# Attention scores in two groups of 64 TensorE columns, with a mask for 16 tokens

## The chip, the cores and the metric

The kernel runs on one core of a Trainium2 chip. The metric is the device time of one execution in microseconds, the median of several runs. The engines are named as in the profile: PE is TensorE, PEld its weight loads, DVE VectorE, ACT ScalarE, POOL GpSimd, SP SyncE (here only a DMA queue).

## The reference

One block on x of shape (8, 1024, 256), float32, so 8192 tokens of width 256. Layer norm gives xn. An attention branch and a mixture of experts (8 experts, the best 2 of each token) both read xn, and the output is x + s * silu(moe). The part that matters here is the attention, which runs over the 4 heads *inside* each token, not over tokens:

```
q = (x @ Wq + bq).reshape(b, s, h, d)      # h = 4 heads, d = 256
k = (x @ Wk + bk).reshape(b, s, h, d)
v = (x @ Wv + bv).reshape(b, s, h, d)
scores = (einsum('bshd,bsgd->bshg', q*cos, k*cos) + einsum('bshd,bsgd->bshg', q*sin, k*sin)) / 16
attn = softmax(scores, axis=-1)            # 4 x 4 numbers for each token
out = einsum('bshg,bsgd->bshd', attn, v)
```

So every token needs 16 dot products of length 512 (cosine and sine part), each between one of its own queries and one of its own keys.

## The kernel before

The tokens go through in 16 quarters of 512 tokens (loop variable `q`, constant `NQ`), the first four (`QE = 4`) ahead of the experts, the other twelve behind them. A quarter has 24 steps `c` on PE. Steps 0 to 15 (L1075, fp32r, 6 matmuls of 512 columns) make the rotated queries and keys. ACT (L814) and DVE (L1590) each write one half of them (cosine, sine) into `QT`, which holds queries as columns (token, head) and keys as columns (head g, token). Steps 16 to 23 (L1086, fp32) make the values folded with Wo, which leave through `u_d` in memory and come back as `US`. Behind the 24 steps come four score groups `n = 4q .. 4q+3` of 128 tokens each (`scores`, L1022), 64 in the kernel.

A score group has four blocks `c` of 32 tokens. In a block the stationary operand is 128 columns of queries (32 tokens times 4 heads), the moving operand 128 columns of keys (4 heads times 32 tokens), in four accumulating fp32 matmuls. Of the 128 x 128 products only those between equal tokens are wanted. DVE multiplies the bank with a mask (`soft_a`, L1478, `maskt` has a one where query row and key column are of one token), sums over the tokens (L1482), takes the maximum and subtracts it (L1483, L1484); ACT takes the exponential (L835); DVE normalises (`soft_b`, L1489 to L1491). In the next quarter `spread` (L1496 to L1505) and `biased` (L1516) get the attention and the values ready, and PE multiplies them in `mix` (L1043: four matmuls, each with 32 stationary columns, one for each 32 PSUM partitions), taken in behind steps 18, 20, 22 and 23.

The score groups alternate between two PSUM banks (`pS`, banks 4 and 5). Group n waits until DVE's mask product of group n-2 is done (`s_sm1`). The steps c go round five banks (`ring`), so step c+5 waits until ACT and DVE have emptied the bank of step c. Each engine works off its own program in order. In quarters 1 to 3 PE also adds up the experts' token lists (`place`, L1053, bf16), POOL and DVE make their operands (L588, L1547, L1551). POOL makes `XTJ` for the next quarter (L574) while the scores run, and behind the experts it also sums the experts' outputs (L658 to L665) and ends with L673 and L674; ACT's silu for it is L801, placed at step 18, and L797 for the quarters of the first half that are finished later. L921 is the router's matmul at the start: 32 stationary columns, 256 moving, one after another. In the last quarter `mix` also follows the scores directly.

Of the kernel before, what the change touches and what calls it, by code (L numbers as in the profile page):

```python
# [9 lines left out]
ALU = mybir.AluOpType  # L10
ACT = mybir.ActivationFunctionType
AX = mybir.AxisListType

NB, S, D, H = 8, 1024, 256, 4
# [22 lines left out]
def program(nc, x, phase, Wq, bq, Wk, bk, Wv, bv, Wo, bo, rw, rb, temp, wg, wp, wo, out):  # L37
    ctx = ExitStack()

    def sb(name, shape, dt=F32):  # L40
        return ctx.enter_context(nc.sbuf_tensor(name, shape, dt))
# [4 lines left out]
    with ctx:  # L46
# [30 lines left out]
        QT = WM[:, 0:16384].rearrange("p (x c n) -> p x c n", x=4, c=2)  # L77
# [14 lines left out]
        TM = sb("TM", [128, 512])  # L92
# [32 lines left out]
        upper = AUX[:, 8064:8192]  # L125
        bo_b = sb("bo_b", [128, D])
        maskt = sb("maskt", [128, 32])
        mask8 = sb("mask8", [128, 8])
        maskr = sb("maskr", [128, 8])
        vec = sb("vec", [128, 4, 8])  # L130
# [28 lines left out]
        SS = sb("SS", [128, 2, 16])  # L159
# [13 lines left out]
        pXT, pS, pD = ps[3], ps[4:6], ps[7]  # L173
# [709 lines left out]
        def _(e):  # L883
# [3 lines left out]
            for k in range(2):  # L887
                mm = e.transpose(bP[:, 32 + 8 * k:40 + 8 * k], rwN[:, 128 * k:128 * k + 128], ident[0:8, 0:8])
# [96 lines left out]
            for j in range(18):  # L985
# [4 lines left out]
                for c in range(2):  # L990
                    if j < 16:
                        k, g = j // 8, j // 2 % 4
                        mm = e.matmul(mb[j % 5][:, :], WvT[:, 2 * g + c, 128 * k:128 * k + 128], wo_r[:, c, :, :],  # L993
                                      start=(c == 0), stop=(c == 1))
                    else:
                        mm = e.matmul(mb[j % 5][0:4, :], bvT[:, c:8:2], wo_r[:, c, :, :],
                                      start=(c == 0), stop=(c == 1))
# [17 lines left out]
            def scores(n):  # L1015
                if n >= 2:
                    e.wait_ge(s_sm1, n - 1)
                for c in range(4):
                    col = 128 * (4 * (n % 4) + c)
                    for x in range(2):  # L1020
                        for h in range(2):
                            mm = e.matmul(pS[n % 2][:, 128 * c:128 * c + 128].rearrange("p (g t) -> p g t", g=H),  # L1022
                                          QT[:, x, h, col:col + 128],
                                          QT[:, 2 + x, h, :].rearrange("p (g t) -> p g t", g=H)[:, :, col // 4:col // 4 + 32],
                                          start=(x == h == 0), stop=(x == h == 1))
                mm.then_inc(s_s, 1)

            def mix(n):
# [160 lines left out]
        def _(e):  # L1189
# [25 lines left out]
            e.wait_ge(s_const, 1)  # L1215
            e.tensor_reduce(maskt[:, :], ident[:, :].rearrange("p (t h) -> p t h", h=H), AX.X, ALU.add)
            ch(e.tensor_reduce(maskr[:, :], ident[:, :].rearrange("p (r a) -> p r a", a=16), AX.X, ALU.add))
            ch(e.tensor_reduce(mask8[:, :], maskt[:, :].rearrange("p (a t) -> p t a", t=8), AX.X, ALU.add))


# [250 lines left out]
            def g4(a, n):  # L1471
                return a[:, n % 2, :].rearrange("p (c g) -> p c g", g=H)

            diag = maskt[:, None, :].broadcast_to([128, 4 * H, 32])

            def soft_a(n):
                e.wait_ge(s_s, n + 1)
                e.tensor_tensor(TM[:, :].rearrange("p (x t) -> p x t", t=32),  # L1478
                                pS[n % 2][:, :].rearrange("p (x t) -> p x t", t=32), diag,
                                ALU.mult).then_inc(s_sm1, 1)  # L1480
                e.wait_ge(s_sm1, n + 1)
                ch(e.tensor_reduce(SS[:, n % 2, :], TM[:, :].rearrange("p (x t) -> p x t", t=32), AX.X, ALU.add))  # L1482
                ch(e.tensor_reduce(sx[:, 0, :], g4(SS, n), AX.X, ALU.max))  # L1483
                e.tensor_tensor(g4(SS, n), g4(SS, n), sx[:, 0, :, None].broadcast_to([128, 4, 4]),  # L1484
                                ALU.subtract).then_inc(s_sub, 1)
# [193 lines left out]
```

## Time and profile before

| | us |
|---|---|
| median of the runs | 1698.37 (1698.24 to 1698.8) |
| the profiled execution | 1698.34 |
| its span in the trace | 1696.6 |
| PE busy | 1643.0 (97%) |
| DVE busy | 988.6 (58%) |
| POOL busy | 785.1 (46%) |
| ACT busy | 733.4 (43%) |
| quarters 0 to 3 | about 128 to 354 |
| experts | about 354 to 1035 |
| quarters 4 to 15 | about 1035 to 1694 |

PE is busy nearly always. A matmul's busy time in the trace goes on beyond its own columns (matmuls overlap in the engine), so what a group of matmuls costs is read from the chain that ended last, or from the distance between starts, and not from the mean of one. An fp32 matmul of the program stands in the trace as two matmuls, each with its own weight load; so 1024 score matmuls are 2048 rows.

### The profile page before, as it was taken

The page shows a single profiled execution, that of the slowest core. Times are in us where ns is not written, and L with a number is a line of the kernel's source. Part 1 is how long each engine was busy: PE and PEld are TensorE (multiplying, and loading weights), DVE is VectorE, ACT ScalarE, POOL GpSimd, SP SyncE. Part 2 cuts the span into 40 slices and gives each one's busy share as a digit, 9 for nine tenths or more (in the row PEclk, how much of TensorE's full clock was granted, in tenths as well). Part 3 has the DMA queues.
Part 4 walks back from the last instruction along what each step waited for, and adds up shares of the span by engine and source line. Part 5 has one row for each costly group of instructions (what it writes and reads, how often), then busy time and mean ns, then how long its engine had stood idle before and what let it go on. Part 6 is the DMA issues. An engine that isn't in the chain of part 4 may idle for free.

```text
span 1696.6 us, 28609 instructions
## 1 busy us (share of the span) xinstructions
PE 1643.0 (97%) x9360; PEld 1276.8 (75%) x9360; DVE 988.6 (58%) x1879; ACT 733.4 (43%) x1205; POOL 785.1 (46%) x945
## 2 busy tenths in 40 slices
PE   5998999989999999999999999999999999999998
PEld 3556676578888888888888888776877668776785
DVE  7568988843333333333333335768777786777766
ACT  5773432513333333333333335355454564535542
POOL 4647577614333433343433442534544646345362
PEclk9999999999999999999999999999999999999998
DMA  9988733162313131313111412424556345552354
GB/s 331 398 319 311 265 107 125 63 263 89 128 51 128 56 124 57 125 57 125 54 54 57 156 54 84 162 101 160 180 180 199 124 155 178 189 182 97 126 168 137
DMA packets 162662, 250.96 MB, mean 148 GB/s; under 512 B 13928, under 2 KB 121248, under 8 KB 161376
## 3 DMA queue, kind: packets, MB, share of 16 engines
q1 hardware_dynamic: 147904, 211.47, 35.8%
q0 software_dynamic: 12960, 35.41, 6.3%
q10 hardware_dynamic: 1664, 2.26, 0.4%
q8 instruction: 88, 1.44, 0.3%
q14 instruction: 46, 0.38, 0.1%
HBM read 149.58 MB, written 99.50 MB: 147 GB/s over the span
## 4 chain that ended last, share of the span: by engine, by line
PE 88%; DVE 6%; DMA 4%; ACT 1%; issue 1%; POOL 0%; ACTq 0%; SPq 0%; DVEq 0%
PE ps L1140 21%; PE ps L1075 19%; PE ps L1022 13%; PE ps L1086 12%; PE ps L1159 10%; PE ps L1149 3%; DMA AUX<-xn_d,AUX 3%; PE ps L1043 2%; PE ps L1122 2%; PE ps L993 2%; PE ps L921 1%; PE ps L911 1%; PE ps L977 1%; DVE WM L1590 1%; DMA WR<-w_d 1%
## 5 line engine op out<-in xcount | busy, mean ns | idle before, releaser
L1140 PE MATMUL ps<-WR,FR 128*128 x1620 | 414.6, 406 | 5.1 <-issue 3.3
L1140 PEld LDWEIGHTS ps<-WR,FR 128*128 128x128 f32 x1620 | 300.7, 192 | 65.6 <-issue 6.7
L646 POOL DMA_INDIRECT y_d<-AUX x135 | 133.7, 990 | 371.6 <-ACT AUX L865 371.6
L1650 DVE TENSOR_TENSOR AUX<-AUX,ps 128x512 f32<-128x512 f32 x135 | 92.9, 688 | 352.7 <-ACT AUX L853 352.7
L814 ACT ACTIVATE WM<-ps,bcs,trig 128x512 f32<-128x512 f32 x256 | 255.7, 1018 | 88.2 <-PE ps L1075 80.5
L1590 DVE TENSOR_SCALAR WM<-ps,vec,trig 128x512 f32<-128x512 f32 x256 | 246.2, 995 | 62.4 <-ACT WM L814 61.8
L1022 PE MATMUL ps<-WM 128*128 128x128 f32 x2048 | 236.3, 277 | 7.2 <-DVE TM L1478 7.2
L1022 PEld LDWEIGHTS ps<-WM 128*128 128x128 f32 x2048 | 232.0, 193 | 14.7 <-DVE TM L1478 8.0
L1086 PE MATMUL ps<-WM,XTJ 128*128 128x512 f32 x512 | 237.1, 600 | 0.0
L853 ACT ACTIVATE AUX<-ps 128x512 f32<-128x512 f32 x135 | 80.9, 599 | 329.0 <-PE ps L1140 329.0
L1159 PE MATMUL ps<-WR,ABR 128*128 x1080 | 209.5, 292 | 0.0
L1075 PE MATMUL ps<-XH,WH 128*128 128x512 f32 x512 | 204.7, 400 | 4.9 <-issue 3.8
L1075 PE MATMUL ps<-XH,WL 128*128 128x512 f32 x512 | 200.3, 391 | 0.0
L1075 PE MATMUL ps<-XL,WH 128*128 128x512 f32 x512 | 200.2, 391 | 0.0
L642 POOL DMA_INDIRECT AUX<-xn_d,AUX x135 | 132.0, 978 | 77.1 <-issue 39.2
L1159 PEld LDWEIGHTS ps<-WR,ABR 128*128 128x128 f32 x1080 | 165.5, 190 | 0.0
L1086 PEld LDWEIGHTS ps<-WM,XTJ 128*128 128x128 f32 x512 | 91.6, 190 | 96.6 <-issue 94.2
L658 POOL TENSOR_TENSOR AUX<-AUX,GP 128x256 f32<-128x256 f32 x128 | 81.9, 677 | 158.1 <-DMA AUX<-in_L_attn_x_dram 155.9
L1159 PE MATMUL ps<-WR,FR 128*128 x540 | 152.0, 281 | 0.0
L821 ACT ACTIVATE UN<-ps 128x512 f32<-128x512 f32 x128 | 76.2, 595 | 138.7 <-PE ps L1086 135.6
L1075 PEld LDWEIGHTS ps<-XH,WH 128*128 128x128 f32 x512 | 96.8, 189 | 25.0 <-issue 4.8
L835 ACT ACTIVATE SE<-SS 128x16 f32<-128x16 f32 x64 | 13.8, 216 | 232.4 <-DVE SS L1484 232.3
(237 smaller groups left out, 2282.5 us busy)
## 6 DMA issues: line engine op xcount, KB each, us to landing
US<-u_d SPq DMA_DIRECT2D x63, 512.0 KB, 4.7
u_d<-UN SPq DMA_DIRECT2D x120, 256.0 KB, 2.0
WR<-w_d SPq DMA_DIRECT2D x8, 3072.0 KB
AUX<-y_d SPq DMA_DIRECT2D x32, 512.0 KB, 5.7
WM<-in_L_attn_x_dram SPq DMA_DIRECT2D x16, 512.0 KB, 9.6
xn_d<-WM SPq DMA_DIRECT2D x32, 256.0 KB, 6.8
w_d<-USR SPq DMA_DIRECT2D x16, 512.0 KB, 5.1
AUX<-xn_d SPq DMA_DIRECT2D x16, 512.0 KB, 6.5
```

The lines of the kernel that those rows point to most:

```text
L642: e.indirect_dma_start(XG[:, m % 2, :], None, xn_d, bass.IndirectOffsetOnAxis(gidx[:, m:m + 1], 0)).then_inc(s_g[m % 2], 16)
L646: e.indirect_dma_start(y_d, bass.IndirectOffsetOnAxis(toks[:, m - 5:m - 4], 0), YS[:, (m - 5) % 2, :], None).then_inc(s_y[(m - 5) % 2], 16)
L658: ins = e.tensor_tensor(y[:, i, :], y[:, i, :], GP[:, i, k, q, None].broadcast_to([128, D]), ALU.mult)
L814: e.activation(rotated(2 * x, i), b, ACT.Identity, bias=bcs[:, x, 0, i:i + 1], scale=trig[:, 0, i:i + 1]).then_inc(s_ca, 1)
L853: e.activation(GR[:, :], mG[m % 2][:, :], ACT.Relu).then_inc(s_gr, 1)
L1022: mm = e.matmul(pS[n % 2][:, 128 * c:128 * c + 128].rearrange("p (g t) -> p g t", g=H), QT[:, x, h, col:col + 128], QT[:, 2 + x, h, :].rea ...
L1075: mm = e.matmul(b[:, :], w[:, k, 128 * c:128 * c + 128], xx[:, k, :], start=(k == 0 and w is WH and xx is XH), stop=(k == 1 and w is WL))
L1086: mm = e.matmul(b[:, :], XTJ[:, k, a // 2, :], M_s[:, k, 512 * a:512 * a + 512], start=(k == 0), stop=(k == 1))
L1140: mm = e.matmul(b[:, :], x, WR[:, bass.ds(off[m] + (2048 * z + 1024 * a + 512 * k), 512)], start=(k == 0 and x is xh and z == 0), stop=(k ...
L1159: mm = e.matmul(mY[m % 2][:, 0:256], x, WR[:, bass.ds(off[m] + (4096 + 1024 * z + 256 * c), 256)], start=(c == 0 and x is hh and z == 0), ...
L1590: e.tensor_scalar(rotated(2 * x + 1, i), ps[bank(24 * q + c)][:, :], bqk[:, x, i:i + 1], trig[:, 1, i:i + 1], ALU.add, ALU.mult).then_inc( ...
L1650: e.tensor_tensor(HS[:, m % 2, :], GR[:, :], mP[m % 2][:, :], ALU.mult).then_inc(s_h, 1)
```

## The change

Each block of 32 tokens is split in two halves of 16 tokens. The stationary operand of a half is 64 query columns, the moving operand 64 key columns (4 heads times 16 tokens), and the result goes to PSUM partitions 0 to 63 for the first half and 64 to 127 for the second, at the same 64 columns. The two halves alternate matmul by matmul. A bank then holds 256 columns of scores in place of 512, the mask has 16 columns in place of 32, and DVE's mask product and sum read 256 columns.

```diff
+        mask16 = sb("mask16", [128, 16])
...
                 for c in range(4):
-                    col = 128 * (4 * (n % 4) + c)
                     for x in range(2):
                         for h in range(2):
-                            mm = e.matmul(pS[n % 2][:, 128 * c:128 * c + 128].rearrange("p (g t) -> p g t", g=H),
-                                          QT[:, x, h, col:col + 128],
-                                          QT[:, 2 + x, h, :].rearrange("p (g t) -> p g t", g=H)[:, :, col // 4:col // 4 + 32],
-                                          start=(x == h == 0), stop=(x == h == 1))
+                            for a in range(2):
+                                row = 64 * a
+                                col = 128 * (4 * (n % 4) + c) + row
+                                mm = e.matmul(pS[n % 2][row:row + 64, 64 * c:64 * c + 64].rearrange("p (g t) -> p g t", g=H),
+                                              QT[:, x, h, col:col + 64],
+                                              QT[:, 2 + x, h, :].rearrange("p (g t) -> p g t", g=H)[:, :, col // 4:col // 4 + 16],
+                                              start=(x == h == 0), stop=(x == h == 1))
                 mm.then_inc(s_s, 1)
...
+            e.tensor_tensor(mask16[:, :], maskt[:, 0:16], maskt[:, 16:32], ALU.add)
...
-            diag = maskt[:, None, :].broadcast_to([128, 4 * H, 32])
+            diag = mask16[:, None, :].broadcast_to([128, 4 * H, 16])
...
-                e.tensor_tensor(TM[:, :].rearrange("p (x t) -> p x t", t=32),
-                                pS[n % 2][:, :].rearrange("p (x t) -> p x t", t=32), diag,
+                e.tensor_tensor(TM[:, 0:256].rearrange("p (x t) -> p x t", t=16),
+                                pS[n % 2][:, 0:256].rearrange("p (x t) -> p x t", t=16), diag,
                                 ALU.mult).then_inc(s_sm1, 1)
...
-                ch(e.tensor_reduce(SS[:, n % 2, :], TM[:, :].rearrange("p (x t) -> p x t", t=32), AX.X, ALU.add))
+                ch(e.tensor_reduce(SS[:, n % 2, :], TM[:, 0:256].rearrange("p (x t) -> p x t", t=16), AX.X, ALU.add))
```

On PE, the score groups of a quarter behind the experts stand between the last `mix` and the first step of the next quarter. Before:

```order
L1043 MATMUL ps<-US,AT 32x256 x3
L1022 MATMUL ps<-WM 128x128 [waits s_sm1,s_cd,s_ca]
L1022 MATMUL ps<-WM 128x128 x15
L1022 MATMUL ps<-WM 128x128 [waits s_sm1]
L1022 MATMUL ps<-WM 128x128 x15
L1022 MATMUL ps<-WM 128x128 [waits s_sm1]
L1022 MATMUL ps<-WM 128x128 x15
L1022 MATMUL ps<-WM 128x128 [waits s_sm1]
L1022 MATMUL ps<-WM 128x128 x15
L1075 MATMUL ps<-XH,WH 128x512 [waits s_ca,s_cd,s_xtd,s_xtc]
```

The same place on PE with the change (line numbers are three higher there):

```order
L1046 MATMUL ps<-US,AT 32x256 x3
L1025 MATMUL ps<-WM 64x64 [waits s_sm1,s_cd,s_ca]
L1025 MATMUL ps<-WM 64x64 x31
L1025 MATMUL ps<-WM 64x64 [waits s_sm1]
L1025 MATMUL ps<-WM 64x64 x31
L1025 MATMUL ps<-WM 64x64 [waits s_sm1]
L1025 MATMUL ps<-WM 64x64 x31
L1025 MATMUL ps<-WM 64x64 [waits s_sm1]
L1025 MATMUL ps<-WM 64x64 x31
L1078 MATMUL ps<-XH,WH 128x512 [waits s_ca,s_cd,s_xtd,s_xtc]
```

Nothing moved: each group has 32 matmuls of 64 x 64 where it had 16 of 128 x 128, behind the same waits.

On DVE, one group's mask product to the end of the softmax of the group ahead of it. Before:

```order
L1478 TENSOR_TENSOR TM<-ps,maskt 128x512 [waits s_s]
L1482 TENSOR_REDUCE SS<-TM 128x16 [waits s_sm1]
L1483 TENSOR_REDUCE sx<-SS 128x4 [waits s_vc]
L1484 TENSOR_TENSOR SS<-SS,sx 128x16 [waits s_vc]
L1489 TENSOR_REDUCE sx<-SE 128x4 [waits s_exp]
L1490 RECIPROCAL sx<-sx 128x4 [waits s_vc]
L1491 TENSOR_TENSOR SA<-SE,sx 128x16 [waits s_vc]
```

The same place on DVE with the change:

```order
L1482 TENSOR_TENSOR TM<-ps,mask 128x256 [waits s_s]
L1486 TENSOR_REDUCE SS<-TM 128x16 [waits s_sm1]
L1487 TENSOR_REDUCE sx<-SS 128x4 [waits s_vc]
L1488 TENSOR_TENSOR SS<-SS,sx 128x16 [waits s_vc]
L1493 TENSOR_REDUCE sx<-SE 128x4 [waits s_exp]
L1494 RECIPROCAL sx<-sx 128x4 [waits s_vc]
L1495 TENSOR_TENSOR SA<-SE,sx 128x16 [waits s_vc]
```

The order is the same, the first two read half as many columns. One small DVE instruction is added at the start of the program (the mask). Nothing changes on ACT, POOL and SP.

## Rows read from the trace of the kernel before

**Rows 1.** The page: busy time, and the chain that ended last.

```profile
PE 1643.0 (97%) x9360; PEld 1276.8 (75%) x9360; DVE 988.6 (58%) x1879; ACT 733.4 (43%) x1205; POOL 785.1 (46%) x945
...
PE 88%; DVE 6%; DMA 4%; ACT 1%; issue 1%; POOL 0%; ACTq 0%; SPq 0%; DVEq 0%
PE ps L1140 21%; PE ps L1075 19%; PE ps L1022 13%; PE ps L1086 12%; PE ps L1159 10%; PE ps L1149 3%; DMA AUX<-xn_d,AUX 3%; PE ps L1043 2%; PE ps L1122 2%; PE ps L993 2%; PE ps L921 1%; PE ps L911 1%; PE ps L977 1%; DVE WM L1590 1%; DMA WR<-w_d 1%
```

**Rows 2.** The chain over one quarter: start us, us, what.

```profile
1131.86 14.49 PE ps L1022 x128
1146.35 21.79 PE ps L1075 x96
1168.14 3.43 PE ps L1086 x8
...
1173.73 0.57 PE ps L1043 x8
```

**Rows 3.** Groups of instructions on PE and PEld, by shape (stationary, then moving).

```profile
L1022 PE MATMUL ps<-WM 128*128 128x128 f32 x2048 | 236.3, 277 | 7.2 <-DVE TM L1478 7.2
...
L1022 PEld LDWEIGHTS ps<-WM 128*128 128x128 f32 x2048 | 232.0, 193 | 14.7 <-DVE TM L1478 8.0 <-issue 5.8 <-ACT UN L821 0.8
...
L1043 PEld LDWEIGHTS ps<-US,AT 128*32 128x32 f32 x504 | 10.1, 108 | 43.1 <-issue 21.2 <-DVE AT L1505 20.8
...
L952 PEld LDWEIGHTS ps<-ident,AUX 128*64 128x64 f32 x3 | 0.3, 110 | 1.7 <-DVE AUX L1339 1.2 <-issue 0.5
```

**Rows 4.** Timeline of PE and PEld around one mix: start us, us.

```profile
1119.95 0.64 PE L1043 MATMUL ps<-US,AT 128*32 128x256 f32 x8
...
1119.94 0.16 PEld L1043 LDWEIGHTS ps<-US,AT 128*32 128x32 f32 x8 [0.76 <-issue]
```

**Rows 5.** The chain at the router and at one place.

```profile
62.41 0.98 PE ps L921 x4
...
224.83 0.24 PE ps L1053 x4
```

**Rows 6.** Timeline of DVE over the quarter of rows 2.

```profile
1142.81 0.69 DVE L1478 TENSOR_TENSOR TM<-ps,maskt 128x512 f32<-128x512 f32 x1 [1.25 <-PE ps L1022]
...
1144.96 0.17 DVE L1491 TENSOR_TENSOR SA<-SE,sx 128x16 f32<-128x16 f32 x1
...
1149.64 3.33 DVE L1590 TENSOR_SCALAR WM<-ps,vec,trig 128x512 f32<-128x512 f32 x3 [0.42 <-ACT WM L814]
```

**Rows 7.** Timeline there, POOL and DVE at once.

```profile
1133.92 4.49 POOL L574 TENSOR_TENSOR XTJ<-XH,XL 128x256 f32<-128x256 f32 x4
...
1137.32 1.13 DVE L1484 TENSOR_TENSOR SS<-SS,sx 128x16 f32<-128x16 f32 x1
```

**Rows 8.** Groups of instructions on DVE.

```profile
L1478 DVE TENSOR_TENSOR TM<-ps,maskt 128x512 f32<-128x512 f32 x64 | 44.2, 690 | 88.1 <-PE ps L1022 88.1
L1482 DVE TENSOR_REDUCE SS<-TM 128x16 f32<-128x512 f32 x64 | 43.9, 686 | 2.2
L1527 DVE TENSOR_TENSOR AUX<-ps,bo_b 128x256 f32<-128x256 f32 x60 | 25.1, 418 | 29.3 <-PE ps L1043 23.5 <-DMA s_d<-AUX 5.6
```

**Rows 9.** The chain at scores of quarters 0, 3 and 15.

```profile
165.45 8.77 PE ps L1022 x64
...
346.82 7.41 PE ps L1022 x64
...
1668.16 7.36 PE ps L1022 x64
...
1680.43 3.78 PE ps L1022 x32
```

**Rows 10.** Busy us (and count) of each engine from 235.3 to 295.6, clock, DMA.

```profile
235.30:295.60 60.30, 60.30 (x370) 42.76 (x370) 53.44 (x110) 23.05 (x30) 49.80 (x51) 1.00 0.26 88
```

**Rows 11.** Timeline of POOL and ACT near step 18.

```profile
1169.21 2.88 POOL L665 TENSOR_TENSOR AUX<-AUX 128x256 f32<-128x256 f32 x4
...
1174.38 1.28 ACT L801 ACT_TABLE_LOAD   x1
```

## The prediction

> **What bounds the kernel now.** I read the page's busy times first: PE is busy for 97% of the span, and 88% of the chain that ended last is PE work, 13% of it the score matmuls [rows 1]. So a microsecond taken from PE counts, unless another engine is right behind. Then the chain over one quarter behind the experts: 14.49 us of scores, 21.79 us of steps 0 to 15, then the fp32 steps with the mixes among them [rows 2]. There is no piece of another engine in it: the quarter of 53.7 us is PE alone, eleven times over. The quarters ahead of the experts are another matter: from 235.3 to 295.6 DVE is busy for 53.44 of 60.3 us [rows 10], and in quarters 0 and 3 only two of the four groups are on the chain [rows 9], since the other two run while DVE does something longer.
>
> **What a score matmul costs.** A quarter has 128 pairs of a weight load and a matmul in 14.49 us, 113.2 ns a pair [rows 2]. Eight matmuls of 512 columns take 3.43 us [rows 2], 0.838 ns a column in fp32. So 128 moving columns stream for 107.2 ns, and 6.0 ns come on top. The weight load is as long as the stream: by its duration, 128 columns take 193 ns and 32 columns 108 [rows 3], 0.89 ns a column over a fixed 80. It lies beside the matmul of the pair ahead, or a pair could not take 113 ns.
>
> **The part that decides: do the two halves run at once?** The change makes 4096 pairs of 64 x 64 out of 2048 of 128 x 128. A half pair streams 64 columns, 53.6 ns, its load is about 57 ns by the same row arithmetic (a 64-column load had 110 ns [rows 3], less still, but that one loads for a transpose). With the 6.0 ns it takes 59.6 ns. One after the other, the 64 pairs of a group take 3.81 us, against 3.62 now: nothing won. Side by side, 32 pair times, 1.91 us: 1.71 us won in each group.
>
> The trace has a matmul split by columns already. A mix is eight pairs on four sets of 32 stationary columns, each with 256 moving columns. One such matmul streams 256 x 0.838 = 214 ns, and the router's matmuls of the same shape, all on one set of columns, take 0.98 us for four [rows 5], or 214 ns each with 0.12 us for the change of shape. Eight in a row would be 1.72 us. The mix takes 0.57 us on the chain [rows 2], its eight loads start within 0.16 us less the 108 ns of the last one, and its matmuls are over in 0.64 us by their modelled ends [rows 4]. So four sets of columns load and stream at once, at almost the full factor (2 x 214 = 428 ns and the change of shape). I take the same for two sets of 64. What it doesn't show is whether this holds for a long stream of pairs (64 a group, where a mix has eight), and with loads as long as the streams (in a mix the load is an eighth of the stream). Bounds for the pair time seen by the group: 28 ns (two at once and nearly no fixed cost, 1.8 us a group) and 59.6 ns (none at once). I take 29.8, nearest to the mix.
>
> A rule of the Trainium skill speaks against the change ("TensorE: Matmul & The Clock Gate", Part 3, what overlaps and what doesn't): weight loads overlap with matmuls in flight only where the row group differs, and here both halves use all rows. By it each load of 53.6 ns would stand outside the streams of all pairs. The rows on the present scores don't agree: PEld is busy for 232.0 us and PE for 236.3 us, together twice the time that the groups take, with all rows in use each time [rows 3].
>
> **DVE.** A mask product and a sum of 512 columns take 690 and 686 ns, a DVE operation from PSUM with 256 columns 418 [rows 8]. So both fall by 0.27 us, 0.54 a group, 35 us of DVE in all, mostly idle time today. For one group with the softmax of the last, DVE goes from 1142.81 to 1144.96 + 0.17 = 1145.13, 2.32 us [rows 6]; it falls to 1.78, still just under PE's new 1.91. But POOL's XTJ work runs for 4.49 us over the scores, and under it a small DVE operation took 1.13 us in place of 0.17 [rows 7]. With one or two such hits DVE ends the four groups about 3 us behind PE; then the evacuations of the next quarter begin. Today the first evacuation ends at 1149.64 + 3.33/3 = 1150.75, 4.4 us behind PE's start of step 0 at 1146.35 [rows 2, 6]. PE waits for it only at step 5, five steps of 21.79/16 = 1.36 us, 6.8 us, on. I expect the 4.4 to become about 5, so PE doesn't wait in most quarters. I take off 0.4 us a quarter for unlucky hits and for the two changes of shape (a change was 0.12 us above).
>
> **The sum**, by what is on the path:
> - Quarter 0: two groups on the chain [rows 9], 2 x 1.71 = 3.4 us. The other two hide behind DVE.
> - Quarters 1 and 2: eight groups, 13.7 us. DVE, 53.44 us busy, saves 2.2 and so has 51.3 us of work in a quarter that would shrink to some 53.4: 1 us each is lost to it. 11.7 us.
> - Quarter 3: two groups on the chain, 3.4 us. The experts: nothing, they only begin earlier.
> - Quarters 4 to 14: 44 groups, 75.3 us, less 11 x 0.4: 70.9 us.
> - Quarter 15: three groups on the chain (7.36 and 3.78 us [rows 9]), 5.1 us, and twice DVE's 0.54 where its softmax stands on the chain: 6.2 us.
>
> Together 95.6 us. The profiled execution took 1698.34 us, 0.03 from the median, so **about 1602 us**, 5.7% less.
>
> **Rivals.**
> *The halves run one after the other.* Then a pair has a fixed cost and 59 groups on the path take 3.81 us in place of 3.62: 11 us more, **1709 us**. The point where it turns is 56.6 ns a pair (3.62 us / 64). For it: the shortest distance between pairs on a whole array is 0.24 us / 4 = 60 ns, at the place matmuls [rows 5]. Against it: the mix. The Trainium skill has a price of this kind ("TensorE: Matmul & The Clock Gate", Part 1, on the missing 2.5 ns): about 62 ns of sequencer time for each matmul where hardware decoding is off. By it a group would take 64 x 62 = 4.0 us and the kernel about 1719 us; the eight loads of a mix that start within some 50 ns [rows 4] don't agree, though a queue filled while PE waited may stand behind that. 11%.
>
> *The halves stream at once but each load stands alone.* A pair of a half is then 53.6 + 53.6 + 6 = 113 ns, two at once, 32 x 113 = 3.62 us a group, as now: **1698 us**, perhaps 1 to 2 less by DVE. The load and stream of the present pairs overlap wholly [rows 3], so 3%. A partial overlap between this and mine, 1650 to 1695, another 4%.
>
> *Another engine becomes the bound.* The quarter shrinks to 46.9 us while DVE, ACT and POOL keep their waits. Two DVE hits more in each quarter put the first evacuation past the 6.8 us, and PE waits 1 to 2 us in each of 14 quarters. POOL's sums ended at 1172.09 and ACT's silu, which needs them, began at 1174.38 [rows 11]: a margin of 2.3 us, and PE's scores will bring step 18 forward by 6.9 us, POOL's inputs (behind ACT's L797, which follows the second softmax) only by about 3. ACT then waits some 1.6 us ahead of step 18's silu in four of the quarters. Steps 16 to 23 go round three banks of 1.72 us each, which should cover it. If it all sticks, 14 x 2 = 28 us of the gain go: **1630 us**. 14%.
>
> *Mine*, 68%: 1590 to 1615. The lower end is a pair time of 28 ns and no waits (59 x 1.8 + 1 = 107 us less), the upper one 1 us more lost in each quarter.
>
> **How the numbers follow.** Mine and the bound by another engine hold 82%; from 1589 to 1640 about 80% of all lies. A measurement can tell about 0.2%, 3.4 us, from no change. Faster by more: 68 + 14 + 4 and half of the 3%, about 87%. Within 0.2%: 2%. Slower: 11%.
>
> **What would show it.** In the chain a quarter's scores should be x256 in about 7.6 us, with pairs in two streams 60 ns apart each; the mean busy of a weight load about 135 ns. The quarter's distance should be about 47 us and PE's waits for DVE L1594 or ACT L815 (the evacuations, by their new line numbers) near nothing. DVE's mask product and sum should be near 0.42 us, and steps 0 to 15 still 21.8 us: if they are longer, the second engine has become late. A granted clock under 1.00 in the scores, where it is 1.00 now [rows 10], would be something I haven't priced. The prediction is wrong at its root if 256 pairs take 14 us or more.

## The result and the profile after

| | us |
|---|---|
| before, four runs on the same chip | 1698.59 (1698.24 to 1705.89) |
| changed | **1608.35** (1603.45 to 1611.25, four runs) |
| ratio | 0.9457, 95% interval 0.943 to 0.9484 |
| the profiled execution, changed | 1606.22, span 1604.5 |

The kernel got 90 us faster where 96 were forecast. The page of the changed kernel, busy times, the granted clock in 40 slices, and the chain that ended last by engine:

```profile
PE 1536.4 (96%) x11408; PEld 1169.5 (73%) x11408; DVE 974.2 (61%) x1880; ACT 730.0 (45%) x1205; POOL 794.2 (49%) x945
...
PEclk9999799989999999999999999999999999999999
...
PE 88%; DVE 5%; DMA 4%; ACT 1%; issue 1%; POOL 0%; ACTq 0%; SPq 0%; DVEq 0%
```

PE is still the bound, with 88% of the chain as in [rows 1], and no other engine has taken its place. The chain over the quarter that answers to [rows 2] (start us, us, what; L1025 is the score matmul, L1078 and L1089 are the steps):

```profile
1108.87 7.62 PE ps L1025 x256
1116.49 21.98 PE ps L1078 x96
1138.47 3.43 PE ps L1089 x8
```

Twice as many pairs in 7.62 us where 14.49 stood: 29.8 ns a pair as the quarter sees it. Steps 0 to 15 take 21.98 us, 0.19 more than before. The groups of the scores and of DVE's two operations on them, beside [rows 3, 8] (engine, operation, shape, count, busy us and mean ns, then idle time ahead and its releaser):

```profile
L1025 PE MATMUL ps<-WM 128*64 128x64 f32 x4096 | 130.9, 227 | 16.2 <-DVE TM L1482 15.6
...
L1025 PEld LDWEIGHTS ps<-WM 128*64 128x64 f32 x4096 | 127.1, 143 | 25.0 <-DVE TM L1482 16.1
```

```profile
L1486 DVE TENSOR_REDUCE SS<-TM 128x16 f32<-128x256 f32 x64 | 26.9, 420 | 2.2
L1482 DVE TENSOR_TENSOR TM<-ps,mask 128x256 f32<-128x256 f32 x64 | 26.8, 418 | 23.0 <-PE ps L1025 23.0
```

The mask product and the sum fell from 690 and 686 ns to 418 and 420, as forecast. What is new is the length of the scores' waits for the mask product: 15.6 us, 7.2 before [rows 3]. The timeline of PE in quarters 0 and 3 shows most of it, in the brackets:

```profile
165.31 6.58 PE L1025 MATMUL ps<-WM 128*64 128x64 f32 x128 [10.46 <-DVE TM L1482]
...
336.08 6.53 PE L1025 MATMUL ps<-WM 128*64 128x64 f32 x128 [4.42 <-DVE TM L1482]
```

and the engines over these two stretches and one of quarter 1 (busy us and count of PE, PEld, DVE, ACT and POOL, then the granted clock, DMA share, GB/s):

```profile
165.30:172.00 6.70, 6.70 (x129) 6.63 (x130) 5.97 (x18) 0.65 (x3) 6.08 (x7) 0.56 1.02 351
336.10:342.60 6.50, 6.50 (x129) 6.43 (x130) 3.89 (x17) 0.65 (x3) 0.41 (x1) 0.56 1.08 442
219.90:221.80 1.90, 1.90 (x64) 1.84 (x64) 0.07 (x1) 0.00 (x0) 1.34 (x2) 1.00 0.58 207
```

After a wait of 10.5 or 4.4 us, 128 pairs take 6.6 and 6.5 us at a mean granted clock of 0.56, mostly the lower level of 1.2 GHz, while 64 pairs in quarter 1 take 1.9 us at 1.00 (2.4 GHz).

Where the time came from, by the start of each quarter's scores in the traces. The second execution is that of the repeat further down:

| stretch | forecast | changed | repeat |
|---|---|---|---|
| to the scores of quarter 1 (quarter 0) | 3.4 | 1.2 | -2.2 |
| quarters 1 and 2 | 11.7 | 9.5 | 11.4 |
| from the scores of quarter 3 to the experts | 3.4 | 0.7 | -4.5 |
| experts | 0 | 4.9 | 3.1 |
| experts' end to the scores of quarter 4 | 0 | 0.0 | 0.0 |
| quarters 4 to 14 | 70.9 | **70.9** | **69.9** |
| quarter 15 | 6.2 | 4.9 | 4.9 |
| sum | 95.6 | 92.1 | 82.7 |

(Before, the scores of quarters 1, 2, 3, 4 and 15 start at 221.0, 279.9, 338.4, 1078.1 and 1668.1; changed, at 219.8, 274.8, 327.7, 1061.8 and 1580.9. The experts, from the start of their first L1140 matmul, L1143 with the change, to the start of the last, run from 359.7 to 1031.3 and from 348.3 to 1015.0.)

### The profile page after: what moved, and what is told of

It is laid out like the page before. It is cut to its first block, busy times and chain, and to the rows that moved or that the text cites. A ratio compares the mean times of both kernels' runs of the same rounds, so it can differ in the third digit from the quotient of the medians.

```text
span 1604.5 us, 32706 instructions
## 1 busy us (share of the span) xinstructions
PE 1536.4 (96%) x11408; PEld 1169.5 (73%) x11408; DVE 974.2 (61%) x1880; ACT 730.0 (45%) x1205; POOL 794.2 (49%) x945
## 4 chain that ended last, share of the span: by engine, by line
PE 88%; DVE 5%; DMA 4%; ACT 1%; issue 1%; POOL 0%; ACTq 0%; SPq 0%; DVEq 0%
PE ps L1143 21%; PE ps L1078 21%; PE ps L1089 13%; PE ps L1162 11%; PE ps L1025 7%; PE ps L1152 3%; DMA AUX<-xn_d,AUX 3%; PE ps L1046 2%; PE ps L1125 2%; PE ps L994 2%; PE ps L922 1%; PE ps L978 1%; PE ps L912 1%; DVE UN L1228 1%; DMA WR<-w_d 1%
## 5 line engine op out<-in xcount | busy, mean ns | idle before, releaser
L1143 PE MATMUL ps<-WR,FR 128*128 x1620 | 408.4, 401 | 5.7 <-issue 3.1
L1143 PEld LDWEIGHTS ps<-WR,FR 128*128 128x128 f32 x1620 | 296.6, 190 | 65.0 <-issue 7.6
L815 ACT ACTIVATE WM<-ps,bcs,trig 128x512 f32<-128x512 f32 x256 | 252.1, 1016 | 89.8 <-PE ps L1078 83.0
L1089 PE MATMUL ps<-WM,XTJ 128*128 128x512 f32 x512 | 237.1, 600 | 0.0
L1078 PE MATMUL ps<-XH,WH 128*128 128x512 f32 x512 | 205.8, 402 | 4.9 <-issue 3.8
L1078 PE MATMUL ps<-XH,WL 128*128 128x512 f32 x512 | 200.5, 392 | 0.0
L1078 PE MATMUL ps<-XL,WH 128*128 128x512 f32 x512 | 200.5, 392 | 0.0
L1089 PEld LDWEIGHTS ps<-WM,XTJ 128*128 128x128 f32 x512 | 91.6, 190 | 96.6 <-issue 92.5
L1162 PE MATMUL ps<-WR,FR 128*128 x540 | 152.0, 281 | 0.0
L1025 PE MATMUL ps<-WM 128*64 128x64 f32 x4096 | 130.9, 227 | 16.2 <-DVE TM L1482 15.6
L1025 PEld LDWEIGHTS ps<-WM 128*64 128x64 f32 x4096 | 127.1, 143 | 25.0 <-DVE TM L1482 16.1
L1078 PEld LDWEIGHTS ps<-XH,WH 128*128 128x128 f32 x512 | 97.0, 189 | 25.8 <-issue 4.9
L1635 DVE TENSOR_TENSOR FR<-ps,FR 128x256 fp32r<-128x256 f32 x135 | 57.3, 425 | 93.2 <-ACT FR L847 93.2
```

The source lines that it names most:

```text
L815: e.activation(rotated(2 * x, i), b, ACT.Identity, bias=bcs[:, x, 0, i:i + 1], scale=trig[:, 0, i:i + 1]).then_inc(s_ca, 1)
L1025: mm = e.matmul(pS[n % 2][row:row + 64, 64 * c:64 * c + 64].rearrange("p (g t) -> p g t", g=H), QT[:, x, h, col:col + 64], QT[:, 2 + x, h, ...
L1078: mm = e.matmul(b[:, :], w[:, k, 128 * c:128 * c + 128], xx[:, k, :], start=(k == 0 and w is WH and xx is XH), stop=(k == 1 and w is WL))
L1089: mm = e.matmul(b[:, :], XTJ[:, k, a // 2, :], M_s[:, k, 512 * a:512 * a + 512], start=(k == 0), stop=(k == 1))
L1143: mm = e.matmul(b[:, :], x, WR[:, bass.ds(off[m] + (2048 * z + 1024 * a + 512 * k), 512)], start=(k == 0 and x is xh and z == 0), stop=(k ...
L1162: mm = e.matmul(mY[m % 2][:, 0:256], x, WR[:, bass.ds(off[m] + (4096 + 1024 * z + 256 * c), 256)], start=(c == 0 and x is hh and z == 0), ...
```

## The experiments

My theory: nearly the whole gain is that the two column halves of the array load and stream at once, and the finer blocks alone bring nothing. DVE's smaller operations matter only where DVE bounds. The first four kernels change the two halves, the next two DVE's part alone, and the rest look into what was left over: the pace, the supply of instructions, and the clock.

**Both halves on one set of columns.**

```diff
-                    for x in range(2):
-                        for h in range(2):
-                            for a in range(2):
+                    for a in range(2):
+                        for x in range(2):
+                            for h in range(2):
...
-                                mm = e.matmul(pS[n % 2][row:row + 64, 64 * c:64 * c + 64]...
+                                mm = e.matmul(pS[n % 2][0:64, 256 * a + 64 * c:256 * a + 64 * c + 64]...
```

> The changed kernel, but both halves go to PSUM partitions 0 to 63 (the second half to columns 256 to 511), so both use the same 64 columns of the array, and the eight pairs of one half of a block stand ahead of those of the other. Partitions 64 to 127 get no scores, so the output isn't the reference's. Theory (the gain is two column sets at once, a pair on one set costs 53.6 + 6.0 = 59.6 ns): 256 pairs of a quarter take 15.3 us in the chain, 0.8 more than the 14.49 before the change, and the kernel about 1700 to 1710 us. Rival (smaller loads and streams overlap better in themselves, the column sets have nothing to do with it): the quarter's scores stay near 7.6 us and the kernel near 1608.

Measured: 1708.99 us (1708.87 to 1715.81), ratio to before 1.0073 (1.0045 to 1.0102). The chain has, for one quarter:

```profile
1243.98 15.07 PE ps L1025 x256
```

58.9 ns a pair, twice 29.4. Same pairs, same shapes, same DVE work, and the 90 us are gone. The edit changes two things, the column set and the order of the pairs; the next run has this order with the two sets kept, and its 9.52 us against 15.07 are the second set alone. So what brings the gain is that a second set of columns runs beside the first. The time is also that of the first rival (1709 us), had the halves not run at once.

**The order of the halves.** First eight pairs of one half and then eight of the other in each block, then all 32 of one half and all 32 of the other in each group.

```diff
                 for c in range(4):
-                    for x in range(2):
-                        for h in range(2):
-                            for a in range(2):
+                    for a in range(2):
+                        for x in range(2):
+                            for h in range(2):
```

(This is the first of the two; the second has `for a in range(2)` ahead of `for c in range(4)` as well.)

> The changed kernel with the loop over the halves outside the accumulation: eight pairs of the first half, then eight of the second, in each block. Theory A (each column set takes its pairs from the queue on its own, as the mixes suggest, where one set's pairs stand next to each other in the program): no difference, 7.6 us a quarter. Rival B (pairs start in program order, so the alternation is what makes them overlap): only the pairs at the seams overlap, 13 to 15.3 us a quarter, the kernel at 1680 to 1710 us.

> The same with the loop over the halves outermost: 32 pairs of the first half, then 32 of the second in each group. Theory A with unlimited view: 7.6 us a quarter. If PE can only look some pairs ahead, the second set starts late in each group and the quarter is between 7.6 and 15.3 us; the start of the second set's first pair against the first set's tells how far it sees. Rival B: 15.3 us.

Measured: by blocks 1636.05 us (1633.95 to 1638.15), ratio 0.963 (0.9597 to 0.9664); by groups 1692.89 (1690.95 to 1699.56), ratio 0.9974 (0.9956 to 0.9991). The chain of one quarter, by blocks and then by groups:

```profile
1215.12 9.52 PE ps L1025 x256
```

```profile
1237.81 13.82 PE ps L1025 x256
```

A quarter has 32 seams between halves in the first kernel and 8 in the second. Against the 15.07 us of one set each seam wins (15.07 - 9.52) / 32 = 0.173 us and (15.07 - 13.82) / 8 = 0.156 us, some three pairs of 59 ns. The single starts say the same: by blocks the second half's first pair starts when the first half has about three pairs left. So here the engine starts a pair of the other set no more than some three or four pairs ahead. By blocks neither expectation came true (7.6 us, or 13 to 15.3); by groups the one of a short view did. Against the kernel before, runs of eight pairs keep 62 of the 90 us and runs of 32 keep 5.5. Two sets of columns run at once all the time only if the program alternates them more finely than that.

**Four sets of 32 columns**, 8 tokens times 4 heads, mask of 8 tokens, 128 columns for DVE.

```diff
-                            for a in range(2):
-                                row = 64 * a
+                            for a in range(4):
+                                row = 32 * a
...
-                                mm = e.matmul(pS[n % 2][row:row + 64, 64 * c:64 * c + 64]...
-                                              QT[:, x, h, col:col + 64],
+                                mm = e.matmul(pS[n % 2][row:row + 32, 32 * c:32 * c + 32]...
+                                              QT[:, x, h, col:col + 32],
...
```

> The split taken one step on: four sets of 32 columns, 8 tokens times 4 heads, mask of 8 tokens (mask8, which is there already), DVE reads 128 columns. A pair streams 32 columns, 26.8 ns, with 6.0 on top 32.8; 32 of them in a row on each of four sets: 1.05 us a group against 1.91, 4.2 us a quarter against 7.62. If nothing else binds, 0.86 us x 59 groups = 50 us off 1608, about 1558 us. Rival (another engine binds): DVE needs about 1.78 - 0.28 = 1.5 us for a group, four groups 6 us and more, so it ends the scores 2 to 3 us later behind PE than now; then PE waits at step 5 and the gain shrinks to 15 to 35 us, 1573 to 1593. Rival (a lowest distance between starts of pairs): with 512 pairs a quarter, at 15 ns each 7.7 us and no gain, 1608.

Measured: 1754.3 us (1745.31 to 1764.78), ratio 1.0332 (1.0298 to 1.0366). Slower than before, and my theory missed it. The chain over one quarter's 512 pairs (of pairs that run side by side it counts only some):

```profile
1264.19 1.43 PE ps L1024 x97
1265.62 2.68 issue
1268.31 1.93 PE ps L1024 x100
1270.23 2.36 issue
1272.60 1.93 PE ps L1024 x102
1274.53 2.64 issue
1277.16 1.50 PE ps L1024 x92
```

The group of these matmuls and the queue of instruction fetches between 1260 and 1285 us (packets, MB, share):

```profile
L1024 PE MATMUL ps<-WM 128*32 128x32 f32 x8192 | 104.0, 216 | 162.6 <-issue 149.2 <-DVE TM L1480 13.3
```

```profile
q8 instruction: 4, 0.07, 1.5%
```

PE stands still for 149 us with nothing that it waits for in the program. By the timeline the bursts are of 163, 128, 128 and 93 pairs. They start 4.29 and 4.56 us apart where they are of 128 pairs (256 instructions). The four fetches are of 16 KB each, which is 64 bytes for each of 256 instructions; they start at 1265.1, 1269.5, 1274.7 and 1279.1, and each burst behind a gap begins 2.5 to 3.2 us after the start of a fetch. Over the whole program this queue moves 88 pieces in the kernel before, 104 in the changed kernel and 136 in this one, one more for every 128 pairs. So a burst is one fetched piece, and the pace is that of the fetches: 4.3 us for 128 pairs in this quarter, 34 ns a pair, slower than the 29.8 ns at which two sets use them up. Over the kernel the next burst starts 3.5 to 7.9 us behind the start of one of 128 pairs, 5.4 in the median. The Trainium skill has the same unit ("Advanced Engine Details and Errata", ISA Cache: 16 KB, 256 instructions), and the trace agrees; it gives no rate of supply.

While instructions are at hand the four sets do what the theory said. The quarter shown and the next one begin at a clock of 1.00:

```profile
1264.01 1.61 PE L1024 MATMUL ps<-WM 128*32 128x32 f32 x163
...
1319.42 2.21 PE L1024 MATMUL ps<-WM 128*32 128x32 f32 x235
```

The 235 starts of the second burst lie within 2.02 us, 8.6 ns a pair, and once they have settled two pairs start every 16.7 ns: 8.3 ns a pair, 33 ns on each of the four sets, where the theory had 32.8. (The expectation of the run with 32 moving columns, below, takes these 16.7 ns for the distance of single pairs; they are that of two.) Behind the gaps of the quarter shown the granted clock is 0.50, and 128 pairs start within 1.69 us, 13.3 ns a pair, 53 ns on a set. So the rival of a lowest distance between pairs did not come true either: the loss is the supply of instructions, and the clock behind the gaps: steps 0 to 15, which follow, take 23.1 to 24.3 us in place of 21.98 in the three quarters from 1109 to 1247.

**DVE's part alone**, both ways: the new matmuls with the old 512 columns for DVE (the diff is of the first, shortened), and the old matmuls with 256 columns for DVE.

```diff
-            diag = mask16[:, None, :].broadcast_to([128, 4 * H, 16])
+            diag = maskt[:, None, :].broadcast_to([128, 4 * H, 32])
...
-                e.tensor_tensor(TM[:, 0:256].rearrange("p (x t) -> p x t", t=16),
+                e.tensor_tensor(TM[:, :].rearrange("p (x t) -> p x t", t=32),
...
```

> The changed PE order, but DVE's mask product and sum go over all 512 columns of the bank with the 32-token mask, as before the change; half of what they read isn't scores of this group, so the output isn't the reference's. It prices DVE's part of the change with the fast PE. Theory (DVE is late at the end of the scores but within the five banks): DVE ends four groups 2.2 us later, 4.4 + about 2.7 us behind PE's step 0, past the 6.8 us in some quarters; 0.5 to 2 us a quarter, 1615 to 1640 us. Rival (DVE has so much room that its part gives nothing): 1606 to 1612.

> The kernel before with DVE's part of the change alone: mask product and sum over 256 columns, PE as before (half of the scores unread, output isn't the reference's). PE bounds the quarters, so DVE's 0.54 us a group counts only where its softmax is on the chain (quarter 15, twice, and quarters 0 to 3): 1695 to 1698 us, 0 to 3 us less than before. If it gave 10 us or more, DVE would have been a second bound all along.

Measured: 1620.08 us (1618.54 to 1628.73), ratio 0.954 (0.952 to 0.956), for the new matmuls alone; 1696.22 (1692.59 to 1704.58), ratio 1.0 (0.998 to 1.002), for DVE's part alone. In the first, the chain of a late quarter is the changed kernel's:

```profile
1222.45 7.62 PE ps L1025 x256
1230.07 22.01 PE ps L1078 x96
```

and the quarters behind the experts stay 47.0 to 48.2 us apart. I had looked for a cost in each of them; there is none, so the margin of DVE behind PE is wider there than I thought. Quarters 1 and 2 take 59.4 and 55.5 us from scores to scores in place of 55.0 and 52.9: 7 us, where DVE's extra work in them is 8 x 0.54 = 4.3 us. That is where DVE bounds. The rest can't be placed: the profiled execution is this kernel's longest (1628.73 us), and 8.5 us of its distance lie in the experts' stage (675.2 us against 666.7), which the edit doesn't touch. By itself DVE's part is worth nothing that can be measured. On top of the new matmuls it is worth some 8 to 12 us between the medians (1620.08 against 1611.62 and 1608.35): the expected total (1615 to 1640) came, but not in the expected place.

**Every score matmul twice** (512 pairs a quarter), to see how far the instructions reach.

```diff
-                for c in range(4):
+                for c in [*range(4)] * 2:
```

> The changed kernel with each group's matmuls issued twice over (same results), so 512 pairs of 64 x 64 a quarter. With two column sets and instructions always at hand: 15.2 us a quarter, 29.8 ns a pair. If the supply of instructions is what gave the kernel with four sets its gaps (about 100 pairs, then 2 to 6 us with nothing to do, 4.4 us and more from run to run of pairs): one 16 KB piece of program holds 128 pairs, and at 4.4 us a piece 512 pairs need 17 to 18 us, with gaps of no named cause behind the first 200 to 300 pairs. Rival (the gaps belong to four column sets): no gaps here.

Measured: 1758.42 us, one run. The chain over one quarter:

```profile
1204.72 10.29 PE ps L1025 x347
1215.02 1.39 issue
1216.41 3.95 PE ps L1025 x128
1220.36 3.63 issue
1223.99 1.32 PE ps L1025 x37
```

347 pairs run through, then PE waits for each piece of 128. At 29.7 ns (10.29 / 347) a piece is used up in 3.95 us, and the next comes 7.6 us after the last. The gaps do not belong to four column sets. The changed kernel asks for 256 pairs and then has long steps: about the size of the reserve. In two of its late quarters PE stops for 0.05 and 0.20 us behind 235 and 251 pairs, and the repeat further down stops at the same two places, for 0.67 and 0.55 us:

```profile
1250.92 7.03 PE ps L1025 x235
...
1258.00 0.85 PE ps L1025 x21
```

**The clock after the long waits.** PE waits in quarters 0 and 3 for DVE. First I filled the wait with repeated scores (group 1 six times, group 13 three times).

```diff
-                for c in range(4):
+                for c in [*range(4)] * {1: 6, 13: 3}.get(n, 1):
```

> The changed kernel, where group 1 is computed six times over and group 13 three times (the same results written again), in the two places where PE waits 10.5 and 4.4 us for DVE with the granted clock at 0.56 behind it. Theory (these waits cost the clock, and with it most of what the change could give in quarters 0 and 3): the 128 pairs behind each wait take 3.8 us in place of 6.58 and 6.53, and the kernel gains 3 to 5.5 us on the changed kernel, about 1603. Rival (DVE is right behind there, so a faster PE only waits for it): the pairs take 3.8 us but the time stays at 1606 to 1611.

Measured: 1625.9 us (1618.85 to 1628.85), ratio 0.9563 (0.954 to 0.9587), slower than the changed kernel. Its chain in quarter 0:

```profile
154.35 5.40 PE ps L1025 x180
159.75 1.64 issue
161.39 3.95 PE ps L1025 x128
165.35 0.60 issue
```

The pairs run at full pace, but their number drains the supply, so the run doesn't tell what the clock alone costs. The scores of quarter 1 come 68.93 us after those of quarter 0, as in the changed kernel (68.90); 12.8 us of what is lost lie in the experts' stage (679.5 us against 666.7), which the edit doesn't touch. Then I filled the waits with few and wide matmuls, 11 and 4 of 512 columns, next to the changed kernel again, unaltered.

```diff
                         scores(4 * q + i)
+                        if i == 1 and q in (0, 3):
+                            e.wait_ge(s_ca, 24 * q + 24)
+                            for _ in range(11 if q == 0 else 4):
+                                e.matmul(ps[0][:, :], QT[:, 0, 0, 0:128], QT[:, 2, 0, 0:512], start=True, stop=True)
```

> The changed kernel once more, beside the next one on the same chip, to have its spread. Its four runs were 1603.45 to 1611.25. Theory: the spread comes from the experts' stage, where the weights of the next expert arrive beside the gathers: each of seven switches delays one or two steps of PE, 666 to 680 us in the profiles so far; the second half should again have quarters of 47.0 to 47.8 us. Median 1603 to 1614.

> The changed kernel with 11 fp32 matmuls of 512 columns behind group 1 and 4 behind group 13, written to a bank that is free there and read by nobody. They fill PE's two waits for DVE with 30 pairs in place of the 832 of the run before, which ran out of instructions (gaps of 1.6, 0.6, 0.3 and 1.7 us) and so mixed two things. Theory: the clock stays up, the 128 pairs behind each wait take 3.8 us in place of 6.5, and without the gaps the kernel is 3 to 5.5 us faster than the changed kernel beside it. Rival: DVE is next there, the 2.7 us turn into waits for DVE behind the scores, and the time is the same within 2 us.

Measured: the changed kernel again 1611.62 us (1605.46 to 1619.97), ratio 0.9481 (0.9451 to 0.9511), as expected, with late quarters of 47.0 to 48.2 us; with the wide matmuls 1622.55 (1617.26 to 1627.95), ratio 0.9556 (0.9535 to 0.9577). The chain of the second in quarter 0, and ahead of the experts:

```profile
168.45 3.95 PE ps L1025 x128
```

```profile
332.80 10.25 DMA AUX<-xn_d,AUX
...
343.59 6.26 PE ps L1065 x32
```

and ahead of the experts in the repeat:

```profile
335.07 10.77 DMA AUX<-xn_d,AUX
...
346.64 6.67 PE ps L1065 x32
```

Neither expectation gave the time: it is neither 3 to 5.5 us less than the repeat's nor the same. In quarter 0 the theory holds: with PE kept at work 128 pairs take 3.95 us at a clock of 1.00 in place of 6.58, and the scores of quarter 1 come 66.2 us after those of quarter 0, not 68.6 to 68.9. In quarter 3 the pairs take 3.95 us too, and nothing is won: PE then waits 3.9 us for the experts' first transfer, the clock is at 0.57 behind it, and L1065 takes 6.26 us. It takes 3.51 us in the changed kernel's first trace, at 1.00. So the wait is only moved, and which of the pieces runs at half clock differs between executions; that is a part of the runs' spread. That the kernel as a whole is 11 us slower in the median is not explained by this: its profiled execution is its fastest (1617.26) and has a span only 1.6 us above that of the repeat's. It stays open.

**The pace of a set.** 32 moving columns in place of 64, and 32 stationary columns in place of 64, one run each.

```diff
-                                mm = e.matmul(pS[n % 2][row:row + 64, 64 * c:64 * c + 64].rearrange("p (g t) -> p g t", g=H),
+                                mm = e.matmul(pS[n % 2][row:row + 64, 64 * c:64 * c + 32].rearrange("p (g t) -> p g t", g=2),
...
-                                              QT[:, 2 + x, h, :].rearrange("p (g t) -> p g t", g=H)[:, :, col // 4:col // 4 + 16],
+                                              QT[:, 2 + x, h, :].rearrange("p (g t) -> p g t", g=H)[:, 0:2, col // 4:col // 4 + 16],
```

```diff
-                                mm = e.matmul(pS[n % 2][row:row + 64, 64 * c:64 * c + 64].rearrange("p (g t) -> p g t", g=H),
-                                              QT[:, x, h, col:col + 64],
+                                mm = e.matmul(pS[n % 2][row:row + 32, 64 * c:64 * c + 64].rearrange("p (g t) -> p g t", g=H),
+                                              QT[:, x, h, col:col + 32],
```

> The changed kernel, but each score matmul moves 32 key columns (two of the four heads g) over the same 64 stationary columns; half of the scores are left out, so the output isn't the reference's. It parts load from stream. Theory (in a pair on one column set the weight load, 64 columns at 0.84 ns and some 5 ns, sets the pace, and the stream lies beneath it): still 58 ns a pair on each set, 7.6 us a quarter. Rival (the stream sets it): about 32 ns a pair on each set, so 4.1 us a quarter, or near 16.7 ns a pair as four sets had it within their runs, 4.3 us.

> The changed kernel, but each score matmul has 32 stationary query columns (the first 8 tokens of each half) and 64 moving ones; half of the scores are left out, so the output isn't the reference's. If the load alone sets the pace it falls to about 32 ns a pair on each set (4.1 us a quarter, if instructions are at hand; with 128 pairs to a piece of 16 KB and 4.4 us a piece, gaps again and some 7 to 9 us). If the stream sets it too, 7.6 us and no gaps.

Measured: 1616.79 and 1600.06 us. A quarter's scores in the chain, moving 32 and then stationary 32:

```profile
1211.13 7.59 PE ps L1025 x256
```

```profile
1202.24 7.14 PE ps L1025 x256
```

Half the moving columns change nothing (29.6 ns a pair, 59.3 for a set), as the theory had it: the load of 64 columns sets the pace there. The stationary run lies between its two expectations. Half the stationary columns bring 6% (27.9 ns, 55.8 for a set), though the mean load of quarters 4 to 15 is shorter by 28 ns (110 against 138): now the stream of 64 sets it. The bursts of the four sets have 32 on both sides, and there a set's pair takes 33 ns at full clock. So in these three shapes and in the changed kernel's a set's pair lasts as long as the longer of load and stream, at the 0.838 ns a column of the prediction (53.6 ns for 64, 26.8 for 32), and 2 to 7 ns more. A shortest distance of some 56 to 60 ns between pairs, whatever the columns, which the two runs by themselves would allow, does not agree with the 33 ns. Two sets with 32 on both sides were not run.

## Why the prediction was right, point by point

**The two halves at once: right.** I had argued it from eight pairs in 0.57 us [rows 2, 4, 5] and took 29.8 ns a pair, 1.91 us a group. Measured: 7.62 / 256 = 29.8 ns, in a stream of 256 pairs with loads as long as the streams. One set of columns gives 15.07 us, which shows the cause. The Trainium skill's rule that I set against it ("TensorE: Matmul & The Clock Gate", Part 3) doesn't hold in these rows: loads and streams that use all 128 rows overlap. What that argument left out is a condition: for the full gain the halves must alternate within three or four pairs. With runs of 32, 13.82 of the 15.07 us stay.

**Fixed cost of 6 ns and the price for each column: right, with a condition.** The sum 53.6 + 6.0 hit the pace of 59.5 ns. The prediction adds the 6 ns to the stream because load and stream are of one length. The longer of the two counts: 59.3 ns with half the moving columns, where the stream alone would give 33, and 55.8 with half the stationary ones. For pairs of 32 x 32 the same sum gives 32.8 ns, and the bursts of four sets have 33. What spoils that kernel, 3.3% slower than before, is a term that the sum doesn't have, the supply of instructions. The Trainium skill ("TensorEngine Tiling (Array Packing)", Theoretical Speedup) gives up to a factor of 4 for a dimension of 32 or less. Within a burst the four sets do run side by side; over the 512 pairs of a quarter no run here shows it, since they take 13 to 19 us against the 7.62 of two sets.

**DVE: right.** Both operations as forecast. The first evacuation of the quarter whose step 0 is at 1116.49 ends at 1120.91 + 5.25/5 = 1121.96, 5.5 us behind it where about 5 were forecast, inside the 6.8 us:

```profile
1120.91 5.25 DVE L1594 TENSOR_SCALAR WM<-ps,vec,trig 128x512 f32<-128x512 f32 x5 [0.16 <-ACT WM L815]
```

There is no wait for an evacuation in quarters 4 to 14. The rival "another engine becomes the bound" did not come true.

**Quarters 4 to 14: right, 70.9 of 70.9**, with the small loss from another source, so that the exact hit is in part luck. I took off 0.4 us a quarter for DVE's unlucky hits and the changes of shape. What is there is 0.19 us a quarter at the change from scores to steps: the steps take 21.98 us in the chain against 21.79, though their own starts keep their distances but for 0.02 us. 21.98 or a little more also stands in the kernels with one set, with the other orders and with DVE's 512 columns, and 21.79 in the one with DVE's part alone, so it goes with the split matmuls. The other part is 2.5 us in all, nearly all of it in three quarters, where PE has gaps of up to 0.7 us called "issue". Those within the scores, behind 235 and 251 pairs, fit the supply of instructions; those ahead of a mix have no cause that I can name.

**Quarters 1 and 2: 9.5 and 11.4 of 11.7.** The allowance for DVE was right in one execution, 2 us short in the other. In both the chain leaves PE for other engines, which before the change it hardly did. In the changed kernel's first trace, between the scores of quarters 1 and 2:

```profile
232.92 1.27 ACT WM L815
...
235.27 3.49 DVE OH L1551
...
270.64 2.65 DMA s_d<-AUX
```

DVE's 53.44 us in [rows 10] had said that this stage has little slack. The 60.3 us of that row are also 1.4 us more than a quarter (58.9 from scores to scores), so the room beside DVE was smaller than the sum took it.

**Quarters 0 and 3: the terms that were mis-sized.** The step was "two groups on the chain, 2 x 1.71 = 3.4 us" for each. Measured: 1.2 and 0.7 us, and less in the repeat. In quarter 0 even the 1.2 is in part chance, since the executions differ by 1.0 and -2.7 us before its scores start; from scores to scores it takes 68.9 and 68.6 us, 69.05 before, so 0.15 and 0.5 us are won. I took each group at the full clock. But the groups that hide behind DVE also got shorter, and DVE's mask product, which ends the wait, comes no earlier: the pairs behind it start at 165.31, and at 165.45 in [rows 9]. So PE waits longer, 10.5 and 4.4 us where it was 6.2 and 1.0, and the 128 pairs behind the wait run at a clock of 0.56: 6.58 and 6.53 us in place of 3.8, 2.7 us lost each time.

In quarter 3 this is nearly the whole of what is missing (3.4 - 0.7). There 7.41 us was near the full pace before, and the trace of before has a clock of 1.00 from 346.8 to 354.2; the fall is new with the change. In the repeat the loss comes behind the scores: 2.9 us of waiting for the experts' first transfer and 6.67 us for L1065, which takes 3.51 at full clock. In quarter 0 a part of the loss was there before: [rows 9] have 64 pairs in 8.77 us, where 64 x 113.2 ns are 7.24. The change brings these scores from 8.77 to 6.58 us, 2.2 won, and 1.1 of it is gone again by the scores of quarter 1 (47.9 us from the end of the one to the start of the other, 46.8 before), in a stage where the chain before stands on DVE for much of the way. The run with wide matmuls in the wait gives 2.6 us back in quarter 0.

**Quarter 15: 4.9 of 6.2.** The step was "three groups on the chain". In the changed trace only the first 128 pairs are on it, 3.91 us, and from 1584.9 on the chain goes by DVE's softmax: the third group hides behind it.

**The experts: 4.9 us that I hadn't counted**, 3.1 in the repeat. It is no merit of the change: over all kernels the stage took 666 to 680 us, 667.4 with the matmuls of before and 679.5 with the new ones. In every trace the steps at the changes of expert are longer, 6.2 to 9.5 us and mostly 7 to 8.5 in place of 4.84, the next one is sometimes at 6.4, and their number differs. Without it the profiled execution would be near 1611, and the two medians of the changed kernel are 1608 and 1612: the gain is some 87 to 90 us by the two comparisons of medians, 91 to 94% of the forecast.

## What to carry to other kernels

Where a product wants only a block diagonal, narrow stationary tiles on separate column sets of TensorE halve the waste. For the full gain the program must alternate the sets nearly matmul by matmul: runs of eight pairs kept 62 of the 90 us, runs of 32 kept 5.5. Count instructions before going finer: in the quarters shown the first 163 to 347 pairs ran without a gap and then 128 came every 4.3 to 7.6 us, so even a stream at 29.8 ns a pair starves once it is long enough. And time won on an engine ahead of a wait for another is not just lost: the longer wait can cost the clock of what comes behind it.

## What the runs showed of the hardware

- Two sets of 64 columns load and stream independently, at 29.8 ns a pair of weight load and fp32 matmul against 58.9 on one set. The second set's first pair starts when the first has some three pairs left.
- On one set a pair lasts as long as the longer of load and stream and a few ns: 59.5 ns with 64 columns on both sides, 59.3 with 32 moving, 55.8 with 32 stationary, 33 with 32 on both (four sets, within a burst at full clock).
- TensorE's instructions come in pieces of 16 KB, 128 pairs here. With 512 pairs a quarter PE was starved for 149 us in the kernel with four sets, and for 39 us with every matmul doubled. Pieces came 3.5 to 7.9 us apart in the first.
- Pairs of 32 x 32 on four sets came 8.3 ns apart at full clock and 13.3 at half clock.
- A wait of 4.4 us ahead of the scores was followed by a granted clock of 0.56 over the next 6.5 us, in a kernel that is at 1.00 nearly everywhere else; in the repeat the same wait was followed by 5.50 us for the same pairs. Eleven matmuls of 512 columns in the wait of quarter 0 kept it at 1.00.
